# A two-layer graph network kernel: one-hots by eight comparisons, merge copies spread, column loads ahead of a wait

## The reference, cut to what matters

```python
# N = 12500 nodes, E = 400000 edges, sorted by dst; 64 features
gauss = exp(sum(-0.5 * (edge_attr - mu)**2 / (EPS + sigma**2)))        # E x 3
msg   = einsum('eko,ek->eo', (x[src] @ g).reshape(E, 3, 64), gauss)
aggr  = segment_sum(msg, dst) / max(cnt, 1)
x     = layernorm(x + silu(aggr + x @ root_w + bias + x))
h     = relu(x @ W_self1 + mean_over_neighbours(x) @ W_neigh1 + b1)
h     = h @ W_self2 + mean_over_neighbours(h) @ W_neigh2 + b2
out   = layernorm(x + h)
```

## Time and profile before

| | |
|---|---|
| median of 3 runs | 7992.47 us (7985.57 to 8002.84) |
| the profiled execution | 8047.77 us, span 8045.9 us |
| PE busy in the span | 5141.5 us (64%) |
| DVE busy | 4379.7 us (54%) |
| ACT busy | 2772.2 us (34%) |
| POOL busy | 3360.0 us (42%) |
| one-hots (L1324) in all | 489, 594.2 us, mean 1215 ns |
| granted TensorE clock, mean | 0.800 |

### The profile page before, as it was taken

One profiled execution on the slowest core, in us unless ns is written; L12 is line 12 of the kernel. 1 busy time (PEld: TensorE's weight loads), 2 busy tenths in 40 slices (PEclk: granted clock), 3 DMA queues, 4 the chain that ended last, 5 costly groups with the idle time before them and its releaser, 6 DMA issues.

```text
span 8045.9 us, 144868 instructions
## 1 busy us (share of the span) xinstructions
PE 5141.5 (64%) x35195; PEld 4042.1 (50%) x35196; DVE 4379.7 (54%) x15088; ACT 2772.2 (34%) x8317; POOL 3360.0 (42%) x3146
## 2 busy tenths in 40 slices
PE   1555555555555555555555555555554699999999
PEld 1223333333444444443334333443443699999999
DVE  5667778766777666655555555555553422222222
ACT  3112333334444444455555555555451100000000
POOL 5013444445666666666666666666650000000000
PEclk5557888877787787777777777777775699999999
DMA  2001111112222222222222222222221399999998
GB/s 68 28 23 56 55 65 65 64 64 68 85 85 85 85 70 86 85 79 75 85 85 76 78 85 85 73 80 85 85 84 42 134 381 382 381 368 385 385 384 346
DMA packets 258352, 1082.32 MB, mean 135 GB/s; under 512 B 140102, under 2 KB 144230, under 8 KB 194406
## 3 DMA queue, kind: packets, MB, share of 16 engines
q1 hardware_dynamic: 142806, 968.66, 31.2%
q0 software_dynamic: 100352, 102.96, 5.6%
q10 hardware_dynamic: 14902, 8.11, 0.5%
HBM read 751.67 MB, written 327.81 MB: 134 GB/s over the span
## 4 chain that ended last, share of the span: by engine, by line
PE 34%; issue 19%; DVE 18%; DVEq 12%; POOL 7%; DMA 4%; ACT 3%; another core or an unknown queue 1%; SPq 1%; ACTq 0%; POOLq 0%
PE pw L965 20%; POOL rE L512 7%; PE pw L795 6%; DVE rE L1264 5%; PE pw L820 3%; DVEq L1297 3%; DVEq L1467 3%; DMA rE<-in_x,idx 2%; DVE rE L1262 2%; DVE rE L1324 2%; PE pw L767 2%; DVE rE L1390 1%; DMA tab<-tab_d 1%; DVE rE L1389 1%; DVEq L1264 1%
## 5 line engine op out<-in xcount | busy, mean ns | idle before, releaser
L512 POOL DMA_INDIRECT rE<-in_x,idx x3136 | 3357.8, 1071 | 2680.9 <-issue 2495.7
L795 PE MATMUL pw<-rE 128*128 128x193 f32 x7824 | 1774.0, 391 | 946.3 <-DVE rE L1324 813.8
L595 ACT CAST rB<-pw 128x792 bf16<-128x792 f32 x1568 | 1252.7, 813 | 3247.8 <-PE pw L820 1081.7
L795 PEld LDWEIGHTS pw<-rE 128*128 128x128 f32 x7824 | 1620.9, 232 | 1163.7 <-DVE rE L1324 983.0
L558 ACT ACTIVATE rE<-rE,cols 128x64 f32<-128x64 f32 x4704 | 1255.0, 344 | 9.3 <-DMA tab<-tab_d 8.2
L820 PE MATMUL pw<-rE 128*128 128x396 f16 x3840 | 822.3, 362 | 669.8 <-DVE rE L1264 471.2
L1264 DVE TENSOR_SCALAR rE<-iperm,gr 128x392 f16<-128x392 f16 x3840 | 1062.3, 317 | 9.7 <-issue 8.8
L820 PEld LDWEIGHTS pw<-rE 128*128 128x128 f16 x3840 | 370.4, 104 | 1060.1 <-DVE rE L1264 547.1
L814 PE MATMUL pw<-rE 128*128 128x396 f16 x1600 | 449.0, 396 | 648.2 <-DVE rE L1390 483.9
L965 PE MATMUL pw<-rB,rA 128*128 128x192 bf16 x9604 | 810.8, 246 | 0.1
L965 PE MATMUL pw<-rE,rA 128*128 128x192 bf16 x9604 | 810.4, 246 | 0.1
(11 more groups left out here) (256 smaller groups left out, 2669.2 us busy)
## 6 DMA issues: line engine op xcount, KB each, us to landing
rA<-count SPq DMA_DIRECT2D x392, 1568.0 KB, 8.4
count<-rB SPq DMA_DIRECT2D x98, 3136.0 KB
rE<-in_x,idx POOLq DMA_INDIRECT x3136
cols<-cols_d SPq DMA_DIRECT2D x98, 64.0 KB
cols_d<-rA SPq DMA_DIRECT2D x3, 1568.0 KB, 5.2
rA<-in_edge_attr ACTq DMA_DIRECT2D x1, 4608.0 KB
out<-gcol ACTq DMA_DIRECT2D x97, 32.0 KB, 6.0
count<-rB SPq DMA_DIRECT2D x8, 224.0 KB, 2.0
```

The source lines that it names most:

```text
L512: pool.indirect_dma_start(out=gath[:, s, u * CB + b, :], out_offset=None, in_=x, in_offset=bass.IndirectOffsetOnAxis(ap=idx[:, s, u * CB + ...
L595: act.copy(stage[:, s, :, j * 2 * W:(j + 1) * 2 * W].rearrange("p h (w n) -> p w h n", w=2), pu[j % 3][:, :, 0:CW].rearrange("p w (h n) -> ...
L795: ins = pe.matmul(sums[side][:, 0:AW], onehot[:, side, bb, :], wgath[:, side, bb, :], start=(bb == 0), stop=(bb == CB - 1))
```

## The change

1. DVE's one-hot L1324, one TENSOR_TENSOR of 1024 elements with two broadcast inputs, becomes eight TENSOR_SCALARs of 128 elements, each against one value per partition of `local`.
2. SP's `after`: the wait for the next tile's gathers and the index load move from first to last place.
3. ACT's 32 copies become four groups of eight, behind units 6 to 9 (in tile 47, whose copies are for the first merged tile, they stay together), and DVE's `merge_ahead` moves from unit 9 to unit 4.

```diff
             def after(part, t, s, last=False, rows=True):
                 base = PARTS[part][0]
-                if rows:
-                    for u in range(U):
-                        sp.wait_ge(a_g[1 - s][u], (t + base + s) * (8 * CB) + 16 * CB)
-                        sp.sem_inc(s_tick[4], 1)
-                    load_idx(t + (base + 3), 1 - s)
                 sp.wait_ge(a_evac, t * NU + (base * NU + NU + 2))
...
                     load_cols(t + (base + 2), s)
+                if rows:
+                    for u in range(U):
+                        sp.wait_ge(a_g[1 - s][u], (t + base + s) * (8 * CB) + 16 * CB)
+                        sp.sem_inc(s_tick[4], 1)
+                    load_idx(t + (base + 3), 1 - s)
...
-            def copied(t, s):
-                act.wait_ge(a_mrg, t * 8 + (2 - 8 * TM))
-                act.sem_inc(s_tick[2], 1)
-                act.load(places, tab[0:1, s * TW_:s * TW_ + T_B0])
-                for j in range(JW):
+            def copied(t, s, part=None):
+                if not part:
+                    act.wait_ge(a_mrg, t * 8 + (2 - 8 * TM))
+                    act.sem_inc(s_tick[2], 1)
+                    act.load(places, tab[0:1, s * TW_:s * TW_ + T_B0])
+                for j in range(JW) if part is None else range(8 * part, 8 * part + 8):
...
-                ins.then_inc(a_mrg, 1)
+                if part is None or part == 3:
+                    ins.then_inc(a_mrg, 1)
...
-                        if merged and j == NU - 4:
+                        if merged == "first" and j == NU - 4:
                             copied(i * 2 + (s + 1), 1 - s)
+                        if merged == "parts" and 6 <= j < 10:
+                            copied(i * 2 + (s + 1), 1 - s, j - 6)
...
-                    V.tensor_tensor(onehot[:, side], iota[:, None, :].broadcast_to([P, CB, P]),
-                                    local[:, :, None].broadcast_to([P, CB, P]),
-                                    ALU.is_equal).then_inc(a_oh[side], 1)
+                    for bb in range(CB):
+                        ins = V.tensor_scalar(onehot[:, side, bb, :], iota[:], local[:, bb:bb + 1], None, ALU.is_equal)
+                    ins.then_inc(a_oh[side], 1)
...
-                        if n == NU // 2 + 1 and not last:
+                        if n == 4 and not last:
                             merge_ahead(t + 1)
```

More of the change, by code:

```diff
@@ L573, in copied, with windows @@
                     ins = act.copy(both[:, :, j], gr[:, bass.ds(at, 2)])
-                ins.then_inc(a_mrg, 1)
-            def windows(i, s, last, merged=False):
+                if part is None or part == 3:
+                    ins.then_inc(a_mrg, 1)
+            def windows(i, s, last, merged=None):
                 act.wait_ge(a_st[s], 16 * i + 1)
@@ L611, in _ @@
             windows(TM // 2 - 1, 0, False)
-            windows(TM // 2 - 1, 1, False, True)
+            windows(TM // 2 - 1, 1, False, "first")
             with act.Fori(0, (NT - TM) // 2 - 1, 1) as i:
                 for s in range(2):
-                    windows(i + TM // 2, s, False, True)
-            windows(NT // 2 - 1, 0, False, True)
+                    windows(i + TM // 2, s, False, "parts")
+            windows(NT // 2 - 1, 0, False, "parts")
             windows(NT // 2 - 1, 1, True)
```

## The result

| | before | after |
|---|---|---|
| median | 7993.40 us (4 runs, 7985.57 to 8002.84) | 8069.12 us (4 runs, 8062.36 to 8072.45) |
| ratio | | 1.0093 (1.0076 to 1.0111) |
| span of the profiled execution | 8045.9 us | 8060.6 us |

The change costs 76 us; the forecast was 30 us less. The profiled execution of before was 55 us above its median.

A forecast was written before the change was run, and what follows sets the result against it. Consumers were taken to set the pace up to about tile 25, POOL's gathers from there. The terms +43 + 7 - 80 = -30 us took 7992.5 to 7962 us, with the forecast case's own range 7930 to 7995.

The forecast's parts named there:

- What bounds the kernel: Aggregation stage: the consumers set the pace up to about tile 25, POOL's gathers from there to the end.
- the sum of busy time, 0.30 and 2.80 us: POOL, tiles 48 to 97: gather time, issue gaps and landing waits sum to 2642 of 2668 us, leaving no consumer waits.
- One-hots, +43 early: DVE up to POOL's takeover: 97 one-hots cost 0.44 us more each, +43 us, bounds 0 and 100.
- One-hots, -80 late: POOL's stage: gathers held less by DVE's shorter comparisons, -80 us, bounds nothing and 108.
- Rival (a): POOL loses every race, a waiting gather kept out to the end of the eight comparisons: 8178 us, 15%.
- the pairing of the forecast: 2259 gathers after 2223 us matched with the DVE instruction they started under; 298 under the wide one-hot lose 107 us.
- The queue: SP's new order: DVE's table waits of 205.9 + 123.7 us go at no gain; index load lands later, +7 us once.
- Cover: POOL: Queue step: a new DVE table wait of up to 5 us a tile is hidden because POOL sets the pace.
- POOL gaps over 3 us: After tile 30, named as a sign that the forecast is wrong, listed beside a period below 50 us for rival (c).
- Index load, +7 once: At POOL's takeover, tile 25: indices land behind store, columns and table, +7 us once, bounds 0 and 11.
- The merge, nothing: Tiles 47 to 97: DVE's 146.5 us wait for the copies goes, all under POOL, so no time changes.
- Changes DVE's waits but not the time, as long as POOL's sum holds: Said of columns not coming early enough for the reordering: no time changes while POOL, never waiting for a consumer, sets the pace.

The follow-up runs named there:

- chips B and C: Two further chips used for follow-up runs; the unchanged kernel before took 8141.76 us on B and 8130.09 us on C.
- O alone: The kernel before with only the one-hots changed to eight comparisons each: 7941.89 us, 0.9933 of before, on the first chip.
- before again: The kernel before, with no edit, run and profiled a second time: 7993.72 us, ratio 0.9996.
- Q alone: The kernel before with only SP's new order, gather wait and index load last: 8151.33 us, ratio 1.0195.

## Why the prediction was wrong, step by step

- **What bounds the kernel** held on the chip of the forecast: consumers up to about tile 25, gathers from there, and the sum of busy time, 0.30 and 2.80 us was complete for the kernel before. It did not hold as a statement on the kernel: on chips B and C the same kernel sits nearer to its other bound.
- **One-hots, +43 early.** The spacing was right (1.57 us for eight). The term was oversized: tile 25 began 20 us later, and tiles 2 to 15 took 69.0 us each in place of 67.5 (forecast 1.8 more); with O alone tile 26 began 30 us later for the consumers, and the rest is presumably hidden in DVE's waits.
- **One-hots, -80 late.** Measured 73 less of POOL's time, within tiles 25 to 97. Rival (a) falls: by the pairing of the forecast, the 211 gathers that start under the new comparisons lose 9.6 us in tiles 48 to 97 of the changed kernel, 0.05 each; in the kernel before, 211 under the wide one lost 77.5. The rule of the Trainium skill (SBUF — State Buffer, "Who interferes with whom"), by which the gain would be nothing or a loss, is not borne out for this form: the long TENSOR_TENSOR holds gathers, the short TENSOR_SCALARs hardly do. The forecast read it for the writing of descriptors alone. The same section also has a DVE instruction with two SBUF inputs contend with a GpSimd instruction that reads SBUF, and these gathers take their row numbers from SBUF (`idx`); with this the trace agrees, as the weighting L1307, a TENSOR_TENSOR of 768 elements, also cost the 132 gathers that started under it 0.34 us each (before again). Together the two terms were -37; measured -54.
- **The queue. This is the step that failed.** It followed the table behind the store and asked who waits for the table, and closed with "Cover: POOL". What it did not ask is what the moved store meets. It took POOL's 2.80 us for landing as fixed, though SP's old wait for gathers was, on this chip, what kept the store off the landings (2 of the 200 gaps with a store over the landing, 45 after the change). The new place, "when the bound is there, in unit 1 or 2 of the tile", is 8.8 us behind a chunk's first gather in 23 of the 50 tiles and some 10.3 in several others, and the same phase comes back from tile to tile (23 times 8.75 to 8.77 us), presumably because the consumers are fed by those gathers. The moved store was priced at nothing and the index load at +7 once; together they cost +74 beside the other parts and +155 alone, where all 50 stores collide. No rival had it. The forecast did name the sign, POOL gaps over 3 us, but for another cause, and as worded it does not separate: the kernel before has 37 and 45 such gaps in its two profiles, the changed one 60. Over 4 us there are 2, 2 and 31.
- **Index load, +7 once.** Seen where it was looked for, but mixed with the collision. POOL starts tile 25 at 2052.99, 9.0 us behind SP's index load at 2043.95 and 12.1 behind the store:

```profile
2040.92 0.37 SPq L398 DMA_DIRECT2D count<-rB  x1
...
2043.95 0.46 SPq L354 DMA_DIRECT2D idx<-idx_d  x1
```

```profile
2052.99 1.23 POOL L512 DMA_INDIRECT rE<-in_x,idx  x1 [9.73 <-ACT rE L558]
```

  With SP's old order and the other parts it starts at 2039, 14 earlier, past the forecast's upper bound of 11. But 7.4 of the 14 lie before tile 24's last gather ended. In the gap of 9.73 most packets of that gather, which ended at 2043.26, start at 2048.7, in the store, and packets of the loads behind it go on to 2051. By an estimate from these times the store over the landing accounts for some 4.5 of the 6.9 us over 2.8, and the index load for the other 2. The ACT instruction that the row names weights a later chunk; the chunk whose buffer POOL needed had been weighted by 2021.3 on ACT and 2042.4 on DVE. With Q alone it was nothing, as the buffers came free no sooner (2017.14 against 2017.13).
- **The merge, nothing.** Wrong with SP's old order (+53 and, on chip B, +28), where the table comes only behind the gathers; beside Q the lag is short (27 us) and the end clean. "Changes DVE's waits but not the time, as long as POOL's sum holds" left out that consumers who fall back are paid for once, behind the last gather.

## What to carry to other kernels

When a DMA is moved, ask what it runs beside at its new place, above all a bulk store beside small gathers whose landing an engine waits for: a wait that looks idle may be what keeps them apart, and only for as long as it is the wait that ends last. A move by which an engine asks for data earlier needs the load to come earlier too, and the lag between producer and consumers, read tile by tile, shows who pays. Where two engines trade the lead, a change that adds to one and takes from the other can change its sign from chip to chip, so measure it on more than one.

## What the hardware showed that was not expected

- A store of 3.1 MB (128 packets, near 0.95 us each, 8.4 us in all) all but shuts out gathers issued from POOL: packets of a gather issued at 4810.26 started in the sixth and seventh microsecond after it, and the landing took 8.61 us in place of 2.8. Over the whole changed kernel, the last packet of a gather starts 1.0 us after POOL is done with it (median), and 4.8 us after when it falls into a store. The Trainium skill (DMA: Bandwidth & Descriptors, "Queues, rings and completion order") has each DMA engine take turns between queues packet by packet, a packet being some 9 to 17 descriptors. If what the profile counts as a packet, one row of 25088 bytes, were such a turn, a gather of one 2048-byte packet on each engine would wait about 1 us, and the trace does not agree: here it waited for some five of eight rows. If a row is one descriptor, an engine's eight rows could be a single turn, and a gather would wait to the end of the store. The trace is nearer to that, with 78 packets in one microsecond as the store ended in the kernel before, but one gather got in ahead of the end there too. No run here settles which.
- The kernel before takes 7996, 8142 and 8130 us on three chips. The profiles taken on them have a granted clock in tiles 2 to 15 of 0.87 on the first and 0.79 to 0.82 on the others, but those on the others are of changed kernels.
